# Attention scores of a decoder layer: three products of rounded halves as one product over 48 stacked rows, stacked through DRAM

## The reference

```
x = x + mixer(layernorm(x))                  # two directions of a state-space scan, fused
x = x + attention(ctx, ctx, layernorm(x))    # 16 heads of 16 features, softmax over 361 keys
x = x + moe(layernorm(x))                    # top 2 of 8 experts, and a shared expert

# attention, per sequence n:
v = values @ Wv.T ; k = keys @ Wk.T ; q = query @ Wq.T       # each (.., 16 heads, 16)
energy = einsum('nqhd,nkhd->nhqk', q, k)
attn = softmax(energy / 16 ** 0.5, axis=-1)
out = einsum('nhqk,nkhd->nqhd', attn, v).reshape(N, Q, 256) @ Wo.T + bo
```

## Time and profile before

| | |
|---|---|
| median of 3 runs | 1074.85 us (1071.8 to 1075.17) |
| the profiled execution | 1072.01 us, of which its span is 1070.3 us |
| PE busy in the span | 971.9 us, 91% |
| DVE busy | 888.1 us, 83% |
| ACT busy | 818.5 us, 76% |
| POOL busy | 681.6 us, 64% |
| mean granted TensorE clock | 0.955 of 2.4 GHz |

### The profile page before, as it was taken

The page is one execution under the profiler, slowest core; times in us unless marked ns, Lnnn a source line. Parts: engine busy times, 40 slices in busy tenths (PEclk is TensorE's granted clock), DMA queues, the critical chain, the costliest instruction groups (busy, mean ns, idle before and its releaser), DMA issues.

```text
span 1070.3 us, 17480 instructions
## 1 busy us (share of the span) xinstructions
PE 971.9 (91%) x6032; PEld 696.0 (65%) x6032; DVE 888.1 (83%) x1027; ACT 818.5 (76%) x1802; POOL 681.6 (64%) x417
## 2 busy tenths in 40 slices
PE   5994898998999989899998999798989989999995
PEld 3543555655656656566565567577767689899995
DVE  7798999999999999999999997666677754665663
ACT  4999999998999999999899851565556655676763
POOL 2001999999999999999999984751120025254442
PEclk9996899999999999999999999899899979999998
DMA  6001344444444434444444432310000009799973
GB/s 196 9 8 45 102 113 111 109 114 110 113 110 110 112 110 113 111 111 112 109 112 111 113 73 68 126 29 15 15 2 2 2 2 334 243 368 324 331 214 57
DMA packets 86775, 122.22 MB, mean 114 GB/s; under 512 B 11127, under 2 KB 79984, under 8 KB 86672
## 3 DMA queue, kind: packets, MB, share of 16 engines
q1 hardware_dynamic: 82848, 115.78, 37.4%
q0 software_dynamic: 3840, 5.34, 2.5%
HBM read 115.92 MB, written 5.99 MB: 114 GB/s over the span
## 4 chain that ended last, share of the span: by engine, by line
PE 40%; DVE 29%; issue 12%; DMA 10%; ACT 7%; POOL 1%; DVEq 0%; POOLq 0%; ACTq 0%
DVE states L1905 16%; PE ps L1337 14%; DMA sums<-y_tile,token_of 9%; PE ps L1229 6%; DVE states L1883 5%; PE ps L1317 4%; PE ps L1212 3%; PE ps L1470 3%; PE ps L1482 2%; DVE neg_max L2021 2%; ACT probs L1099 2%; PE ps L1498 1%; PE ps L1325 1%; PE ps L1222 1%; PE ps L1517 1%
## 5 line engine op out<-in xcount | busy, mean ns | idle before, releaser
L743 POOL TENSOR_TENSOR states<-states,c_row 128x800 f32<-128x800 f32 x255 | 473.2, 1912 | 89.4 <-DVE states L1905 89.1
L1337 PE MATMUL ps<-states,ident 128*128 128x400 f32 x1024 | 381.0, 508 | 11.4 <-DVE u L1913 11.4
L1337 PEld LDWEIGHTS ps<-states,ident 128*128 128x128 f32 x1024 | 186.9, 192 | 116.7 <-DVE u L1913 12.7
L1905 DVE TENSOR_TENSOR_SCAN states<-sb_decay,ps 128x800 f32<-128x800 f32 x128 | 231.9, 1812 | 4.7 <-ACT sb_decay L1013 3.9
L1905 DVE TENSOR_TENSOR_SCAN states<-ps,states 128x800 f32<-128x800 f32 x128 | 230.2, 1798 | 1.1 <-ACT ps L1013 1.1
L1005 ACT ACTIVATE xT<-xn_tok,xT 100x256 f32<-100x256 f32 x512 | 216.4, 493 | 0.6 <-PE ps L1317 0.2
L1013 ACT ACTIVATE ps<-dt,neg_a 128x396 f32<-128x396 f32 x256 | 141.2, 583 | 45.1 <-DVE states L1905 44.2
L1317 PEld LDWEIGHTS ps<-ident,xT 100*128 100x128 f32 x1024 | 101.1, 145 | 81.2 <-issue 62.8
L1013 ACT ACTIVATE sb_decay<-dt,neg_a 128x396 f32<-128x396 f32 x256 | 144.4, 611 | 1.0 <-DVE states L1905 0.9
L1317 PE MATMUL ps<-ident,xT 100*128 100x100 f32 x1024 | 114.8, 257 | 29.4 <-DVE states L1905 17.6
L1099 ACT ACTIVATE probs<-ps,neg_max 100x361 f32<-100x361 f32 x128 | 70.9, 560 | 65.0 <-DVE neg_max L2021 64.4
(11 more groups left out here) (273 smaller groups left out, 1643.6 us busy)
## 6 DMA issues: line engine op xcount, KB each, us to landing
c_row<-rows SPq DMA_DIRECT2D x256, 200.0 KB, 3.1
w_tile<-in_w SPq DMA_DIRECT2D x40, 1024.0 KB
b_row<-rows SPq DMA_DIRECT2D x32, 200.0 KB, 3.1
ctx<-in_ctxT SPq DMA_DIRECT2D x8, 361.0 KB, 3.9
win<-in_winT SPq DMA_DIRECT2D x2, 1024.0 KB, 10.9
shared_raw<-in_w SPq DMA_DIRECT2D x2, 1024.0 KB, 6.6
wout<-in_woutT SPq DMA_DIRECT2D x2, 512.0 KB, 6.5
token_rows<-rows_src SPq DMA_DIRECT2D x1, 828.1 KB
```

Source lines behind the costliest of these rows:

```text
L743: nc.gpsimd.tensor_tensor(st, st, c_row[i % C_SLOTS][:].unsqueeze(1).broadcast_to([P, CP, TQ]), ALU.mult).then_inc(product_ready, 1)
L1337: mm = nc.tensor.matmul(ps[:, j, 0:TQ], ident[:], states[i % RING][:, j * TQ:(j + 1) * TQ], start=(n == 0), stop=(n == N - 1), skip_group_ ...
L1905: nc.vector.tensor_tensor_scan(st, rates, inflows, 0.0, ALU.mult, ALU.add).then_inc(scan_done, 1)
```

## The change

**Stacking.** The three products of one head have 16 rows each. They are put under each other: for the keys the 48 rows are (high, high, low), for the queries (high, low, high), so that one product over 48 rows gives high x high + low x high + high x low. `scores` now has 2 matmuls for a group instead of 6, one for each head, on rows 0 to 47 and 64 to 111.

**Through DRAM.** The stacked layout crosses partitions, so it is made by DMA. SP stores the high keys twice and the low keys once into k_rows (`store_keys`: 6 DMAs per batch, 8 heads x 16 rows x 362), and the same with the queries (`store_queries`: 6 DMAs for each half). Then POOL issues 2 DMAs (`load_stack`), one for even and one for odd heads, that bring 48 rows x 8 heads x 362 into k_stack (q_stack for queries). k_stack and k_rows have two slots; kT_h and kT_l now have one. The scores of a batch wait for k_stacked instead of the copies of the keys.

**Order.** The keys of batch b+2 are now made from g = 7 of batch b (half 0) and g = 0 of batch b+1 (half 1); the values of b+1 at g = 3 and 4. Keys and values of batches 0 and 1, and all queries, are made before the loop, in other PSUM banks; ACT copies the values of batch 0. The scores of groups 0 and 1 come after all of these. wo is loaded in 8 DMAs of 16 partitions, in another head order, and the weights of the values are split by POOL in 4 instructions instead of 2. The mask of the queries and its second copy go, so do the zeros behind the probabilities; the last tile of the turned probabilities has 105 rows instead of 128.

**POOL's queue.** The loads stand in POOL's stream between the context splits: for batch 2 ahead of the splits of the shared weights, for every later batch ahead of the split of the next context. The bias add, the routing constants and the shared weights come later than before.

The core of the diff:

```diff
-MASS_AT, PROJECT_AT, KEYS_AT, VALUES_AT = 1, 2, (3, 4), (5, 6)
+MASS_AT, PROJECT_AT, VALUES_AT = 1, 2, (3, 4)
...
+KEYS_HIGH, KEYS_LOW, QUERIES_HIGH, QUERIES_LOW = (0, 1), 2, (0, 2), 1
+FIRST_BATCHES = 2
...
+        def keys_at(b, g):
+            if g == GROUPS - 1 and b + 2 < B:
+                return b + 2, 0
+            if g == 0 and 1 <= b < B - 1:
+                return b + 1, 1
+            return None
...
+            def store_part(rows, parts, at, signal):
+                for m in range(KD):
+                    heads = rows[m * HT:(m + 1) * HT, at * HD:(at + 1) * HD, :]
+                    sp.dma_start(heads, parts[:, m, :].bitcast(F32)).then_inc(signal, 16)
+
+            def store_keys(b):
+                r = b % 2
+                if b >= 2:
+                    sp.wait_ge(k_stacked[r], 16 * 2 * (b // 2))
+                sp.wait_ge(k_high, KD * (b + 1))
+                for at in KEYS_HIGH:
+                    store_part(k_rows[r], kT_part[0], at, k_stored[0][r])
+                keys_copied(sp, b, KD - 1)
+                store_part(k_rows[r], kT_part[1], KEYS_LOW, k_stored[1][r])
...
+            def load_stack(to, rows, signal):
+                for i in range(2):
+                    nc.gpsimd.dma_start(to[block_rows(i)], rows[i::2].rearrange("t r s -> r t s")).then_inc(signal, 16)
+
+            def stack_keys(b):
+                r = b % 2
+                if b >= 2:
+                    pool.wait_ge(scores_ready, GROUPS * (b - 1))
+                pool.wait_ge(k_stored[0][r], 16 * 4 * (b // 2 + 1))
+                pool.wait_ge(k_stored[1][r], 16 * 2 * (b // 2 + 1))
+                load_stack(k_stack[r], k_rows[r], k_stacked[r])
...
+            for b in range(3, B):
+                stack_keys(b)
+                if b + 1 < B:
+                    split_context(b + 1)
...
             def scores(b, r, g):
-                m = 2 * g // HT
-                if g % (GROUPS // KD) == 0:
-                    pe.wait_ge(k_copied, 2 * b + (m + 1))
-                if not isinstance(b, int) or GROUPS * b + g >= 2:
+                if g == 0:
+                    pe.wait_ge(k_stacked[r], 16 * 2 * (b // 2 + 1))
+                    if b % BQ == 0:
+                        pe.wait_ge(q_stacked[b // BQ], 16 * 2)
+                if GROUPS * b + g >= 2:
                     pe.wait_ge(probs_ready, 2 * GROUPS * b + (2 * g - 2))
-                for n, (hi, lo) in enumerate(((0, 0), (0, 1), (1, 0))):
-                    for i in range(2):
-                        _, j, par = head_at(2 * g + i)
-                        rows = slice(j * QUAD, (j + 1) * QUAD)
-                        mm = nc.tensor.matmul(ps[0:L, g % 2 * 2 + i, 0:SE],
-                                              q_part[par][hi][rows, m, b * L:(b + 1) * L],
-                                              kT_part[r][lo][rows, m, :], start=(n == 0), stop=(n == 2))
+                for i in range(2):
+                    mm = nc.tensor.matmul(ps[0:L, g % 2 * 2 + i, 0:SE],
+                                          q_stack[block_rows(i), g, b * L:(b + 1) * L],
+                                          k_stack[r][block_rows(i), g, :], start=True, stop=True)
...
+            pe.wait_ge(kv_split, 6 + 4)
+            for m in range(KD):
+                keys(0, m)
             turn_x2(0)
+            values(0, 1)
             queries(0)
-            pe.wait_ge(kv_split, 4 + 4)
-            for m in range(KD):
-                keys(0, 0, m, FIRST_KEYS[m])
+            values(0, 0)
             turn_x2(1)
             for m in range(KD):
-                job_copied(pe, ("qT", m, 0))
-            pe.wait_ge(k_copied, KD)
-            scores(0, 0, 0)
-            scores(0, 0, 1)
+                keys(1, m)
+            queries(1)
             for k in range(KD):
                 job_copied(pe, ("xn2T", k, 1))
-            for part in range(2):
-                values(0, 0, part, FIRST_VALUES[part])
-            queries(1)
-            pe.wait_ge(v_copied, 2)
+            scores(0, 0, 0)
+            keys_copied(pe, 1, KD - 1)
+            scores(0, 0, 1)
+            for part in (1, 0):
+                values(1, part)
```

More of the change, by code:

```diff
@@ L475, in decoder_layer @@
         y_gated = sem("y_gated")
-        probs_zeroed = sem("probs_zeroed")
-        mask_ready = sem("mask_ready")
+        q_stored = [sem(f"q_stored{q}") for q in range(Q)]
+        k_stored = [[sem(f"k_stored_{n}{r}") for r in range(2)] for n in ("high", "low")]
+        q_stacked = [sem(f"q_stacked{q}") for q in range(Q)]
+        k_stacked = [sem(f"k_stacked{r}") for r in range(2)]
         v_zeroed = sem("v_zeroed")
@@ L647, in _ @@
             sp.dma_start(b2_sb[:], b2).then_inc(moew_in, 16)
+            for b in range(FIRST_BATCHES, B):
+                store_keys(b)
+                if b + 2 < B:
+                    load_context(b + 2)
             sp.wait_ge(route_consts, ROUTE_CONSTS)
@@ L754, in split_into @@
                 high, low = part
-                ones_of = one[:].unsqueeze(2) if len(raw.shape) == 3 else one[:]
+                ones_of = one[:]
+                for _ in raw.shape[2:]:
+                    ones_of = ones_of.unsqueeze(2)
                 nc.gpsimd.tensor_tensor(high, raw, ones_of.broadcast_to(raw.shape), ALU.mult).then_inc(done, 1)
@@ L777, in _ @@
             for b in range(2):
-                split_context(b, b, 1)
-            for r in range(2):
-                nc.gpsimd.memset(probs[r][:, :, S:], 0.0).then_inc(probs_zeroed, 1)
+                split_context(b)
+            stack_keys(0)
+            stack_queries(0)
             pool.wait_ge(xn_ready, (1 + DIRS + 1) * B)
@@ L2013, in copy_values @@
+            def copy_values(b, part):
+                size, tiles = ((P, (0, 1)), (SL, (2,)))[part]
+                if b < FIRST_BATCHES:
+                    job_result(dve, ("v", b, part))
+                    src, done = bank(("v", b, part)), copied["v"]
+                else:
+                    dve.wait_ge(v_done, 2 * (b - FIRST_BATCHES) + part + 1)
+                    src, done = ps[:, KEY_BANK, :], v_copied
                 for n, kt in enumerate(tiles):
-                    to = v_sb[r][0:size, kt].rearrange("p h (c e) -> p h c e", e=HD)[:, :, 0:VW // HD:2, :]
@@ L2101, in _ @@
             dve.wait_ge(v_zeroed, 2)
-            for part in range(2):
-                copy_values(0, 0, part, FIRST_VALUES[part])
-            for m in range(KD):
-                low_queries(m, 1)
+            for part in (1, 0):
+                copy_values(1, part)
             for b in range(B):
```

288 lines of the change are left out of this document (188 added, 100 removed).

## The result

The changed kernel takes 1148.44 us (median of four runs, 1147.66 to 1148.53) against 1075.01 for the kernel before on the same chip: a ratio of 1.0664, with an interval of 1.0635 to 1.0692. The profiled execution took 1147.7 us, 1.8 beyond its span of 1145.9. So the sign was forecast rightly, the size was not: +25.5 us were forecast, and +73 came.

A forecast was written before the change was run, and what follows sets the result against it. No engine was saturated within a group; each group was a ring of scores, maxima, exponentials, turning. Start +7.4, batches +19.1 and end -1 gave +25.5 us, 1097.5 profiled, forecast 1100 us, range 1064 to 1118.

The forecast's parts named there:

- S(2): Attention loop: the moment when the first scores of batch 2 start; the number in brackets is the batch.
- 384 / 16 x 78 ns = 1.9 us of moving: Loads into the stack: moving time of 384 rows over 16 engines at 78 ns a packet, within 5.9 us for two loads.
- POOL's issue: Stack loads: POOL's time to issue one load, taken as 1.3 us, between 0.38 and 3.0.
- R: Round trip of the keys through DRAM, wakes, stores and loads: 15.1 us, from 13.3 to 18.5 on 8 engines.
- Ring: Attention loop, from a batch's first scores to the next batch's high keys: 9.3 us, plus 1.1 for the lower clock.
- the forecast batch of 25.5: Attention loop: 9.3 us plus R of 15.1 is 24.4, with 1.1 for the clock 25.5 us a batch.
- The start: Before batch 1's first scores: the queries' trip delays the first turning to 699.2, batch 1's scores come 7.4 us later.
- The product: Scores: two pairs of products fewer, 0.33 us a group, 2.6 us a batch; a batch without wait taken as 20.0 us.
- Behind S(7): After the first scores of batch 7: the groups lose some 0.1 us each, -1 us.
- A: Rival: round trip hidden, stores on 16 engines or at twice the rate, batches of 20.0 us, 1062 us; chance 0.22.
- C: Rival, slower still: POOL's load issue at 3.0 us, 1124 us, or clock staying at 1.2 GHz, 1120; chance 0.15.
- B: Rival: no change, R about 12.5 us with cheap loads and stores better than 8 engines, 1075 us; chance 0.05.

The follow-up runs named there:

- e6: Changed kernel with the same key-load packets sent to all 128 partitions instead of 48 (rows in wrong places): 1116.8 us, one execution.
- e1: Changed kernel with the key loads from batch 2 on issued by SP on its hardware queue instead of POOL on the software queue: 1135.2 us.
- e12: Changed kernel with the stores of batch 1's keys and context load 3 issued only when the first queries are loaded: 1150.6 us.
- e8: Changed kernel with each head's DRAM rows padded from 48 to 64, one load over 128 partitions replacing two over 48: 1129.0 us.
- e11: Kernel before with the high halves' score product made three times in place of the three different products: 1077.6 us.
- e3: Changed kernel without key stores and stack loads from batch 2 on, computing instructions kept (output not the reference's): 1081.1 us.
- e4: Kernel before with only the high halves' product in the scores, two matmuls a group instead of six: 1076.1 us.
- e9: Changed kernel with the round trip by halves, one padded load per half, and batch 1's key stores held back until the first queries are loaded: 1093.5 us.
- e10: As e9, but each pair of score products is made three times over into the same place: 1094.7 us.
- by halves: Changed kernel with each half of keys and queries stored, loaded and waited for by itself, same bytes and queues: 1085.5 us.
- e2: Changed kernel with DRAM rows grouped by part, each store writing 128 rows in sequence, three loads per block instead of one: 1137.8 us.

## Why the prediction was wrong in its size

- **The sign and the mechanism** were right: the trip through DRAM stands exposed at S(2) to S(7), the stores use 8 engines (0.50 in the window at 776), the clock falls to 1.2 GHz in each wait, and no engine waits for a computing row of POOL's list.
- **The step that failed: "384 / 16 x 78 ns = 1.9 us of moving" for a load.** It took the 78 ns of a packet from a load over 128 partitions for a load over 48. The loads took 10.1 us instead of 5.9; POOL's issue, the uncertain term of that step, was cheap (1.28 us for two, 2.6 taken), and the moving, which seemed certain, was the dear one. 4.2 us in each of six batches are 25 of the missing 50. With all partitions written (e6) the same packets took 5.7 us, close to the forecast's 5.9. The range of R (13.3 to 18.5) could not hold 19.6 (9.5 + 10.1), since its ends came from the issue alone and none from the moving.
- **The rest of a batch.** Ring 11.0 against 10.4, stores 9.5 against 9.2: with the loads the forecast batch of 25.5 becomes the 30.6 of S(2) to S(3). S(2) - S(1) was 29.5 against 23.2. Of these 6.3 us the loads are 4.3 once more, and 1.8 are the ring (9.9 us from S(1) to the first store against 8.1): S(1) found the clock down (0.62 us a score matmul at 730.40), where I had reckoned with the full clock. In e1 S(1) found it up, and the ring took 8.1 us (725.24 to 733.34).
- **The start: +23.6 against +7.4.** The queries' trip was costed as if they had the queues to themselves but for six stores. The second high half was ready at 682.2 (ACT's q_h at 681.70) instead of 677; from the first queries' store at 682.80 to their loads 15.0 us passed instead of 8.7; the loads took 13.2 instead of 5.9. A slip of 0.8 us is in the sum: the queries' stores were given 0.5 us from moving to landing (688.6 to 689.1), the keys' 1.3. Of the rest e12 puts 1 to 2.5 us down to the stores of batch 1 in the way, and e8 shows that the width of the loads does not mend it by itself: its one load of the queries over 128 partitions took 14.4 us (696.97 to 711.34). The start is the mis-sized term next to the loads; which transfer beside it costs the rest stays open. Why the first split is 5 us late was not tried; about 2 us of it are the mixer, whose last scan ends at 640.9 instead of 638.6, but it ends at 640.9 with the kernel before too (e11). The profiles of the same start in e1 and e3 have S(1) 5 to 6 us earlier, so the 16 us of this term are uncertain by that much.
- **The product.** At full clock it was worth 1.3 us a batch (e4, batch 6) and 1.5 (e9 against e10), where 2.6 was the upper bound and the forecast took 1.4 of it (21.4 to 20.0): rightly sized. What the forecast left out is that the clock falls oftener with fewer products, also without any wait; in e4's profile the falls take more from the loop than the products give. The 20.0 us of e3 are a mean of batches of 18.8 to 19.4 us at full clock and of 20.9 to 21.0 with a dip, so that the mean fits is in part luck. With three products and the new order a batch at full clock takes 20.95 us (e10) against 21.4 before: about 0.5 us come from the other edits (keys half a step earlier, values over two groups, turned tiles of 105 rows instead of 128); which of them was not tried.
- **Behind S(7):** -1 forecast, +3.2 measured; the clock is down behind the wait at 910.84 (0.62 us a score matmul), but this part differs by 5 us between the kernel before and e11, which change nothing there, so no cause is shown.
- **The rivals.** A (hidden) fell with the stores at 0.50. C named a dearer trip, but by POOL's issue at 3.0 us (0.64 measured) or by a clock that stays down (it rose after each wait), and priced it at 1124. B's 12.5 us was far off.
- **The rule of the Trainium skill** that the prediction cites (DMA: Bandwidth & Descriptors, anatomy of one DMA) gave 4.5 us for both loads. The trace disagrees by 5.6 us (10.1); with all partitions written it is 5.7 in all (e6), 1.2 above the rule.

The missing 50 us are so made up in the two profiles: loads in the loop 25, start 16, the rest of the six batches 5 (29.7 less 25), and 4 behind S(7). The first is shown by an experiment that takes it away (e6). The 4, and 5 to 6 of the 16, are within what profiles of the same code differ by.

None of the versions beats the kernel before. The best with the right output, by halves, is 1.0% behind it, and without any trip in the loop the kernel is as far behind. In the latter what remains is the start alone; by halves, in its profile, it is the start (S(1) 15.8 us later than before) and the loop with its stretches at 1.2 GHz (8.0 us). No start without its trip was tried.

## What to carry to other kernels

Price a DMA by the nearest row that writes or reads the same number of partitions, not the same packet size: 48 partitions took 130 GB/s where 128 took 400. When one late piece holds a wait for the whole, split the signal by what its first user needs, before making the transfer faster: halves gave 60 us here, wider loads 19, wider stores 11. And before PE work is traded for a wait, take the work away alone: four of six matmuls a group were worth 1.3 us a batch at full clock and nothing in the whole time, since the granted clock fell in five of six batches instead of one. When two such versions come out alike, compare batches at the same clock first.

## What the runs showed of the hardware

- The same 768 packets of 1.4 KB: share 1.7 on the software queue and 1.1 on the hardware queue at the same 130 GB/s. A queue's share of engine time is no measure of its cost when the destination is the limit.
- POOL issues a plain load of 384 rows in 0.64 us; about 1.4 us pass until its first packets move (in e8 from 776.61 to the window of 778).
- With fewer matmuls and no new wait on PE the mean granted clock was lower, 0.933 to 0.945 against 0.947 to 0.957, and PE ran at 1.2 GHz while its row shows it busy for the whole of the window. A batch of one kernel took 19.4 us at full clock, 20.9 with 3.4 us at 1.2 GHz, and 23.8 with 10.2 us (e3, e9).
- SP's issue of a store on 8 engines is dearer, and dearer still when many are queued: six in 4.4 us in the loop (770.96 to 775.32), against six in 2.8 us in e2, where each store is spread over 16 engines; at the start of the changed kernel, behind six of the queries and five of its own batch, a single one took 2.1 us (694.05).
